# A GRU's first 20 steps take their input products on TensorE, and one prune moves from GpSimd to VectorE

## The chip, the cores and the metric

One core of one Trainium2 chip runs the whole program. The metric is device time of one execution in microseconds (us). The engines are named as in the profile: PE is TensorE (PEld its weight loads), DVE VectorE, ACT ScalarE, POOL GpSimd, SP SyncE; each runs its own queue of instructions in order and waits on semaphores that the others raise.

## The reference

Two blocks of attention and feed-forward; the change lies where the first block's feed-forward meets the GRU (a recurrent cell) of the second. `x` has 4 sequences (B) of 256 tokens (S) with 256 features (D).

```python
# first block's feed-forward, 2-of-4 sparse; I = 1024
h = silu(x @ w_gate) * (x @ w_up)
out = sparsify_2to4(h) @ w_down        # in each four, the two largest |h| stay
x = x + out
# GRU over the 256 tokens; state h: [4, 256]
gi = x_t @ W_ih + b_ih                 # depends on x alone: "input products"
gh = h @ W_hh + b_hh                   # depends on the step before
r = sigmoid(i_r + h_r); z = sigmoid(i_z + h_z); n = tanh(i_n + r * h_n)
h = (1 - z) * n + z * h                # 256 steps, one after the other
```

The attention and the routed feed-forward that follow are not touched.

## The kernel before

The feed-forward and the GRU run together. The tokens are cut into 8 tiles of 32 steps (each tile has 32 tokens of each of the 4 sequences). A tile goes through these stages, and each must be done before the GRU reaches the tile:

- `hidden_in(tile, n, up)`: gate (up = 0) or up product of half n (512 of the 1024 hidden features), two matmuls of 512 columns, into one of the PSUM banks a to d.
- `gate_sigmoid`, `gate_copy`, `up_copy` (ACT), then `multiplied` and `pruned`/`pruned_pool`: silu times up, then the 2-of-4 mask. In tile 0 DVE does it (`multiplied_at_once`, `pruned`). In tile 1 POOL multiplies both halves; DVE prunes the first half just before the GRU begins and POOL the second. In later tiles POOL does all of it.
- `by_hidden` (PE transposes), `by_hidden_out` (ACT copies them), `down` (PE, product with w_down), `grown` (DVE adds to xT, the tokens by feature).
- `rows_in` (PE): the tile's input products for r and z, by token; `rows_out` (DVE) adds the biases and writes them to SBUF; `spread`: 16 DMAs a tile move them into `g_row`, one row per step, in the layout that the steps want. SP issues 8 of tile 0's and ACT 8; of a later tile SP issues 12 and ACT 4. `cols_in` and `cols_out` do the same for n without DMAs.

Tile 0's stages, up to the landing of its 16 DMAs, stand in front of step 0. Those of the later tiles are fitted into the steps: after a step's three gates PE has one slot for an extra piece of work, and a step without such a piece has one `keep_warm` matmul there. DVE and ACT have such slots too. Which step has which piece is written out by the step's place u in its tile.

A step t, with what releases what:

- ACT has copied ("seeded", L1408) the input products of r and z and the bias of n into three banks. PE adds h @ W_hh (`gate`, L1324): for each of r, n, z 8 small matmuls (weights of 4 columns, 64 moving columns, four column groups side by side), 16 records in the profile, 48 a step.
- DVE transposes r (L1620), then n (L1624); ACT takes the sigmoid of r (L1448), then of z (`gate_z`, L1453), and then seeds r for the step after (`seed_r`). DVE: pre_n (L1629), transpose of z (L1631). ACT: tanh (L1457), then it seeds n and z (`seed_nz`), then its own extra piece. DVE: h (L1638), which releases PE's next step.

At a tile's first step `seed_r` waits until the tile's 16 DMAs have landed (g_g2).

## Time and profile before

| | us |
|---|---|
| median of 3 runs | 1009.99 (1008.89 to 1012.1) |
| profiled execution, its own time | 1006.44 |
| its span, first to last instruction | 1004.5 |
| PE busy | 798.6 (79%) |
| DVE busy | 609.5 (61%) |
| ACT busy | 477.3 (48%) |
| POOL busy | 414.2 (41%) |

The mean granted TensorE clock over the span is 0.962 of full speed. The busy shares are means over stages with different limits; in the GRU, which runs from 326.65 to about 815 us, no engine is full, and what counts is the loop from h to the next h. Times in the rows are us from the start of the span.

### The profile page before, as it was taken

Reading aid. Unit: us, or ns where it says so; the run is one execution under the profiler, and the core shown is the slowest. Engines: PE = TensorE matmul, PEld = TensorE weight load, DVE = VectorE, ACT = ScalarE, POOL = GpSimd, SP = SyncE. Lnnn points to the kernel's source line nnn. Section 1 sums busy time; section 2 is a strip of 40 time slices with the busy share of each in tenths; the row PEclk is TensorE's granted clock in tenths of the full one; section 3 lists DMA queues with packets and bytes.
Section 4 is the critical chain, followed back from the end, with each engine's and each line's share of the span. In section 5 each row is a group of like instructions: output and inputs, shape, how many; then the busy total and the mean of one; then the engine's idle time right before and its main releaser. Section 6 shows DMA issues by size and latency. Waiting matters only on the chain.

```text
span 1004.5 us, 39546 instructions
## 1 busy us (share of the span) xinstructions
PE 798.6 (79%) x16646; PEld 511.5 (51%) x16646; DVE 609.5 (61%) x2100; ACT 477.3 (48%) x1905; POOL 414.2 (41%) x493
## 2 busy tenths in 40 slices
PE   3789977868997886969779696886776678998876
PEld 3444544445654564645546464564544445566554
DVE  5655555786647676666767666676666643334347
ACT  2523433376642565656556565565544523344222
POOL 0385680374136394773928659095002002220000
PEclk9999999998999999999999999899989989999968
DMA  8100000400000000000000000000031000000001
GB/s 254 31 1 2 1 1 1 157 1 1 2 22 11 4 8 11 3 15 5 12 6 4 14 4 14 4 4 15 4 84 48 4 2 1 2 2 1 1 1 42
DMA packets 33343, 20.14 MB, mean 20 GB/s; under 512 B 23952, under 2 KB 30096, under 8 KB 33168
## 3 DMA queue, kind: packets, MB, share of 16 engines
q1 hardware_dynamic: 27984, 17.04, 6.1%
q8 instruction: 131, 2.15, 0.9%
q10 hardware_dynamic: 5184, 0.59, 0.4%
q14 instruction: 44, 0.36, 0.1%
HBM read 14.47 MB, written 1.05 MB: 15 GB/s over the span
## 4 chain that ended last, share of the span: by engine, by line
PE 52%; DVE 24%; ACT 8%; issue 6%; SPq 2%; DMA 2%; POOL 1%; ACTq 0%; DVEq 0%; POOLq 0%
PE banks L1324 15%; PE banks L1269 5%; DVE work L1624 4%; DVE h_ring L1638 3%; DVE gate_r L1620 3%; PE banks L1294 3%; ACT nzh L1457 3%; DVE pre_n L1629 3%; SPq L1249 2%; PE banks L410 2%; PE banks L1668 2%; PE banks L385 2%; PE banks L318 2%; PE banks L1750 2%; PE banks L1724 1%
## 5 line engine op out<-in xcount | busy, mean ns | idle before, releaser
L1324 PE MATMUL banks<-w_qkv,h_ring 128*4 128x64 f32 x12288 | 228.4, 224 | 111.9 <-DVE h_ring L1638 100.2
L1324 PEld LDWEIGHTS banks<-w_qkv,h_ring 128*4 128x4 f32 x12288 | 179.1, 89 | 214.9 <-DVE h_ring L1638 199.5
L1448 ACT ACTIVATE banks<-gate_r 128x8 f32<-128x8 f32 x256 | 46.2, 181 | 182.5 <-DVE gate_r L1620 181.7
L1620 DVE STREAM_TRANSPOSE gate_r<-banks 128x64 f32<-128x64 f32 x256 | 63.9, 250 | 80.2 <-PE banks L1324 76.3
L318 PE MATMUL banks<-zero 128*128 128x512 bf16 x285 | 97.8, 413 | 3.4 <-DVE work L2196 2.6
L1624 DVE STREAM_TRANSPOSE work<-banks 128x64 f32<-128x64 f32 x256 | 76.6, 299 | 2.7 <-PE banks L1324 2.5
L1638 DVE TENSOR_TENSOR_SCAN h_ring<-banks,nzh 128x24 f32<-128x24 f32 x256 | 52.9, 207 | 34.3 <-ACT nzh L1457 2.8
L1489 POOL TENSOR_TENSOR work<-work 128x512 f32<-128x512 f32 x14 | 17.8, 1270 | 122.8 <-ACT work L1385 122.8
L1629 DVE TENSOR_TENSOR_SCAN pre_n<-banks,work 128x16 f32<-128x16 f32 x256 | 48.7, 190 | 27.3 <-DVE work L1624 1.4
L1631 DVE STREAM_TRANSPOSE banks<-gate_z 128x64 f32<-128x64 f32 x256 | 60.4, 236 | 4.8 <-ACT gate_z L1453 3.7
L1457 ACT ACTIVATE nzh<-pre_n 128x8 f32<-128x8 f32 x256 | 54.5, 213 | 16.2 <-DVE pre_n L1629 1.4
L1453 ACT ACTIVATE gate_z<-banks 128x64 f32<-128x64 f32 x256 | 57.4, 224 | 9.3 <-PE banks L1324 9.3
L1565 POOL COPY probs_b<-h_ring 128x128 f32<-128x128 f32 x16 | 7.3, 486 | 125.5 <-DVE h_ring L1638 125.5
L1408 ACT COPY banks<-big 128x64 f32<-128x64 f32 x256 | 53.9, 211 | 9.8 <-DMA big<-big 9.8
L1408 ACT COPY banks<-grids 128x64 f32<-128x64 f32 x256 | 53.9, 211 | 0.8 <-DMA grids<-big 0.8
L1133 DVE TENSOR_REDUCE nraw<-banks 128x2 f32<-128x512 f32 x64 | 42.3, 686 | 19.3 <-PE banks L816 19.1
L1408 ACT COPY banks<-bhn 128x64 f32<-128x64 f32 x256 | 53.9, 211 | 0.0
L1588 DVE TENSOR_TENSOR nzh<-h_ring,banks 128x16 f32<-128x16 f32 x256 | 43.8, 171 | 11.0 <-ACTq L1444 1.8
L318 PEld LDWEIGHTS banks<-zero 128*128 128x128 bf16 x285 | 28.2, 102 | 38.3 <-issue 9.5
L1903 ACT ACTIVATE work<-banks 128x768 f32<-128x768 f32 x32 | 24.2, 808 | 38.0 <-PE banks L1750 38.0
L1294 PE MATMUL banks<-work,shared 128*128 128x128 f32 x256 | 36.4, 287 | 0.7 <-ACT work L1397 0.7
L645 POOL TENSOR_TENSOR rq<-nrm,half 128x64 f32<-128x64 f32 x3 | 31.7, 10577 | 12.0 <-DVE nrm L695 12.0
(436 smaller groups left out, 1654.1 us busy)
## 6 DMA issues: line engine op xcount, KB each, us to landing
big<-in_x SPq DMA_DIRECT2D x1, 1024.0 KB, 5.8
w_gate<-in_L_ffn_w_gate SPq DMA_DIRECT2D x1, 1024.0 KB, 5.0
shared<-in_L_ffn_w_down SPq DMA_DIRECT2D x1, 1024.0 KB, 7.5
w_gate<-in_L_ffn_W SPq DMA_DIRECT2D x1, 1024.0 KB, 7.4
shared<-in_L_ffn_W SPq DMA_DIRECT2D x1, 1024.0 KB, 11.3
out_x<-big SPq DMA_DIRECT2D x4, 256.0 KB, 2.4
w_qkv<-in_L_cond_W_qkv SPq DMA_DIRECT2D x1, 768.0 KB, 7.0
w_qkv<-in_L_attn_W_qkv SPq DMA_DIRECT2D x1, 768.0 KB, 8.7
```

What stands on the lines that cost most here:

```text
L318: nc.tensor.matmul(bank[:, :], zero16[:, 0:P], zero16[:, :], start=True, stop=True, skip_group_check=True)
L1269: mm = nc.tensor.matmul(bank[:, :], xg[:, tile, k, :], w_gate[:, k, n * 512:(n + 1) * 512] if not up else w_up[2 * k + n], start=(k == 0), ...
L1294: mm = nc.tensor.matmul(out[:, 0:P], w_down[:, c, m * P:(m + 1) * P], keptT[:, c, :], start=(c == 0), stop=(c == FC - 1), skip_group_check ...
L1324: mm = nc.tensor.matmul(bank[32 * j:32 * j + B, 0:64], h_col(t, c), w_hh[:, c, g, :].rearrange("p (m n) -> p m n", m=KC)[:, :, 32 * j:32 * ...
L1408: return nc.scalar.copy(bank[:, 0:64], rows).then_inc(done, 1)
L1453: nc.scalar.activation(gate_z[:, :], bank_z[:, 0:64], ACT.Sigmoid, scale=-1.0).then_inc(g_sz, 1)
L1457: nc.scalar.activation(every(nzh[:, :], 0, 3), every(pre_n[:, :], 1), ACT.Tanh, scale=-1.0).then_inc(g_th, 1)
L1620: nc.vector.transpose(gate_r[:, :], bank_r[:, 0:64]).then_inc(g_tr, 1)
L1624: nc.vector.transpose(blocks(npair[:, 16 * (t % RING):16 * (t % RING) + 128], 0), bank_n[:, 0:64].rearrange("p (m n) -> p m n", m=KC)).the ...
L1629: nc.vector.tensor_tensor_scan(pre_n[:, :], zr[:, :], npair[:, 16 * (t % RING):16 * (t % RING) + 16], 0.0, ALU.mult, ALU.add).then_inc(g_p ...
L1631: nc.vector.transpose(blocks(zz[:, :], 2, 3), gate_z[:, :].rearrange("p (m n) -> p m n", m=KC)).then_inc(g_tz, 1)
L1638: nc.vector.tensor_tensor_scan(h_ring[:, h_at(t + 1):h_at(t + 1) + 24], zz[:, 0:24], nzh[:, :], 0.0, ALU.mult, ALU.subtract).then_inc(g_h, 1)
```

## The change

Steps 0 to 19 (`DIRECT = 20`) no longer take their r and z input products from `g_row`. ACT seeds their banks with the bias alone (`bias_row`, four small DVE copies made once), and PE adds x_t @ W_ih with a new function, `inputs`: 8 matmuls of the same shape as a gate's, with token t's columns of xT as weights. For z they stand between gate n and gate z of the same step. For r they stand after gate z of the step before, ahead of the step's extra piece. So tile 0's `rows_in` move into the slots of steps 0 and 1, its `rows_out` to steps 3 to 6, and its 16 `spread` DMAs are all issued by SP; step 20 is the first that waits for them.

Tile 1's first half is now multiplied and compared on DVE before `grown`, counted after it, and its four last operations (`kept_of`) stand in steps 0 to 3. POOL multiplies and prunes only tile 1's second half, and not before h of step 0 is ready (g_h). The extra pieces of tile 0's steps are newly set: `by_hidden(1)` in steps 4 and 12, `hidden_in(2)` in 6 to 11, 13 and 14, and `down(1)`, `grown(1)`, `rows_in(1)`, `cols_in(1)`, `rows_out(1)` and tile 1's `spread` one step later than before (`late`). There are no keep_warm matmuls in steps 0 to 18 nor the 24 before step 0.

```diff
+            def inputs(t, bank, g, seed):
+                pe.wait_ge(seed, t + 1)
+                for c in range(KC):
+                    for j in range(4):
+                        nc.tensor.matmul(bank[32 * j:32 * j + B, 0:64], xT[:, c, t:t + (B - 1) * S + 1:S],
+                                         w_ih[:, c, g * D:(g + 1) * D].rearrange("p (m n) -> p m n", m=KC)[:, :, 32 * j:32 * j + 32],
+                                         start=False, stop=False, skip_group_check=True)
...
-            for k in range(KC):
-                rows_in(0, k)
-            cols_in(0)
+            pe.wait_ge(e_x2, 2)
             for bank in (bank_r, bank_n, bank_z):
                 mm = nc.tensor.matmul(bank[:, 0:64], zero16[:, 0:P], zero16[:, 0:64], start=True, stop=True, skip_group_check=True)
             mm.then_inc(g_open, 1)
-            keep_warm(24, bank_b)
+            cols_in(0)
+            inputs(0, bank_r, 0, g_sdr)
...
                 gate(t, bank_n, 2, g_sdn, g_nm)
+                if t < DIRECT:
+                    inputs(t, bank_z, 1, g_sdz)
                 gate(t, bank_z, 1, g_sdz, g_zm)
-                if u in (3, 4) and tile + 1 < TILES:
+                if t + 1 < DIRECT:
+                    inputs(t + 1, bank_r, 0, g_sdr)
+                if tile == 0 and u in (0, 1):
+                    rows_in(0, u)
+                elif tile == 0 and u in (4, 12):
+                    by_hidden(1, u // 12)
+                elif tile == 0 and u in (6, 7, 8, 9):
+                    hidden_in(2, 0, u // 8, [u % 2])
+                elif tile == 0 and u in (10, 11, 13, 14):
+                    hidden_in(2, 1, u < 12, [u - (10 if u < 12 else 13)])
...
-                else:
+                elif t + 1 >= DIRECT:
                     keep_warm(1, bank_b)
...
+            def row_of(t, g):
+                if t < DIRECT:
+                    return bias_row[:, 2 * g:2 * g + 2, :].rearrange("p m n -> p (m n)")
+                return g_row[t // TILE % 2][:, t % TILE, g, :]
...
             def seed_r(t):
-                if t % TILE == 0:
+                if t == DIRECT or t and t % TILE == 0:
                     act.wait_ge(g_g2, G2_DMAS * 16 * (t // TILE + 1))
...
-            for n in range(2):
-                multiplied(pool, nc.gpsimd, chain, 1, n)
+            pool.wait_ge(g_h, 1)
+            multiplied(pool, nc.gpsimd, chain, 1, 1)
             pruned_pool(pool, chain, 1, 1)
...
+            multiplied_at_once(v, chain, 1, 0)
+            compared(v, chain, 1, 0)
             for m in range(KC):
                 grown(0, m)
-            for n in range(4):
-                rows_out(0, n)
...
+            counted(chain, 0)
...
+                if tile == 0 and u < 4:
+                    kept_of(0, u)
+                if tile == 0 and u in (3, 4, 5, 6):
+                    rows_out(0, u - 3)
...
-                for j in range(2 if tile == 0 else 3):
+                for j in range(4 if tile == 0 else 3):
```

## Rows read from the trace of the kernel before

**Rows 1.** The page's costliest group: the gates (busy, mean ns of one | idle before).
```profile
L1324 PE MATMUL banks<-w_qkv,h_ring 128*4 128x64 f32 x12288 | 228.4, 224 | 111.9 <-DVE h_ring L1638 100.2
```

**Rows 2.** Timeline of PE ahead of step 0: start, length, what [idle <-releaser].
```profile
306.25 1.95 PE L1294 MATMUL banks<-work,shared 128*128 128x128 f32 x16
309.63 0.66 PE L1282 MATMUL banks<-cst,work 128*128 128x128 f32 x4 [1.43 <-DVE work L1512]
310.97 2.05 PE L1294 MATMUL banks<-work,shared 128*128 128x128 f32 x16 [0.68 <-ACT work L1397]
...
315.26 1.16 PE L1316 MATMUL banks<-xT,w_ih 128*128 128x128 f32 x8
...
326.65 1.46 PE L1324 MATMUL banks<-w_qkv,h_ring 128*4 128x64 f32 x48 [4.97 <-ACT banks L1408]
```

**Rows 3.** Timeline of DVE in the same stretch.
```profile
296.51 0.43 DVE L1501 TENSOR_SCALAR work<-work 128x512 int32<-128x512 int32 x1
...
297.45 0.42 DVE L1504 TENSOR_TENSOR c2p<-work 128x256 bf16<-128x256 f32 x1
...
298.20 0.49 DVE L1506 TENSOR_TENSOR win<-c1p 128x512 bf16<-128x512 bf16 x1
...
300.02 1.30 DVE L1512 SCALAR_TENSOR_TENSOR work<-win,work 128x128 f32<-128x128 bf16 x4
...
302.68 1.45 DVE L1501 TENSOR_SCALAR work<-work 128x512 int32<-128x512 int32 x1
...
304.64 1.49 DVE L1504 TENSOR_TENSOR c2p<-work 128x256 bf16<-128x256 f32 x1
...
313.06 0.29 DVE L1577 TENSOR_TENSOR xT<-banks,xT 128x128 f32<-128x128 f32 x1 [0.60 <-PE banks L1294]
```

**Rows 4.** Timeline of POOL: the first of tile 1's two multiplies.
```profile
302.57 1.27 POOL L1489 TENSOR_TENSOR work<-work 128x512 f32<-128x512 f32 x1 [9.52 <-ACT work L1385]
```

**Rows 5.** Timeline of ACT: the first seed.
```profile
326.30 0.22 ACT L1408 COPY banks<-big 128x64 f32<-128x64 f32 x1 [9.10 <-DMA big<-big]
```

**Rows 6.** Timeline, all engines: a step with keep_warm (step 5).
```profile
336.97 0.86 PE L1324 MATMUL banks<-w_qkv,h_ring 128*4 128x64 f32 x48 [0.40 <-DVE h_ring L1638]
...
337.76 0.39 PE L318 MATMUL banks<-zero 128*128 128x512 bf16 x1
337.89 0.22 ACT L1453 ACTIVATE gate_z<-banks 128x64 f32<-128x64 f32 x1
...
338.81 0.86 PE L1324 MATMUL banks<-w_qkv,h_ring 128*4 128x64 f32 x48 [0.66 <-DVE h_ring L1638]
```

**Rows 7.** Timeline, all engines: a step whose gate_z came late (step 70).
```profile
459.03 0.86 PE L1324 MATMUL banks<-w_qkv,h_ring 128*4 128x64 f32 x48 [0.65 <-DVE h_ring L1638]
...
460.14 0.22 ACT L1453 ACTIVATE gate_z<-banks 128x64 f32<-128x64 f32 x1 [0.17 <-PE banks L1324]
460.26 0.22 ACT L1408 COPY banks<-big 128x64 f32<-128x64 f32 x1
...
461.02 0.39 PE L1324 MATMUL banks<-w_qkv,h_ring 128*4 128x64 f32 x13
```

**Rows 8.** Timeline of PE: extra pieces down (step 14) and rows_in (step 19).
```profile
354.67 1.16 PE L1294 MATMUL banks<-work,shared 128*128 128x128 f32 x8
355.76 0.86 PE L1324 MATMUL banks<-w_qkv,h_ring 128*4 128x64 f32 x48
...
363.90 1.04 PE L1306 MATMUL banks<-w_ih,xT 128*32 128x512 f32 x8
```

**Rows 9.** Timelines of SP and ACT: tile 1's DMAs and the seed waiting for them.
```profile
372.83 10.44 SPq L1249 DMA_DIRECT2D grids<-big  x12
...
386.74 0.22 ACT L1408 COPY banks<-grids 128x64 f32<-128x64 f32 x1 [0.31 <-DMA grids<-big]
```

**Rows 10.** Windows (length, busy by engine, PEclk the granted clock): step 62, steps 0 to 19.
```profile
443.30:445.70 2.40, 2.00 (x49) 1.28 (x49) 1.36 (x7) 0.95 (x7) 2.32 (x4) 0.51 0.00 0
...
326.65:365.06 38.41, 34.34 (x1029) 22.16 (x1029) 25.58 (x123) 23.55 (x130) 21.73 (x28) 0.95 0.02 4
```

More of the change, by code:

```diff
@@ L1260, in hidden_in @@
                         pe.wait_ge(e_free, n + 1)
+                    elif tile == 2 and n == 0:
+                        pe.wait_ge(e_free, 3)
                     elif tile and up == 0:
@@ L1275, in by_hidden @@
                 pe.wait_ge(e_kept[n], tile + 1)
[L1276 removed]
+                if tile == 1 and n:
+                    pe.wait_ge(e_trc, 3)
+                elif tile and n == 0:
                     pe.wait_ge(g_nd, tile)
@@ L1354, in phase3_pe @@
                 tile, u = divmod(t, TILE)
+                late = 1 if tile == 0 else 0
                 pe.wait_ge(g_h, t + 1)
@@ L1444, in phase3_act @@
             act.sem_inc(g_act, 1)
+            for m in range(KC):
+                cols_out(0, m)
             for t in range(S):
                 tile, u = divmod(t, TILE)
+                late = 1 if tile == 0 else 0
                 act.wait_ge(g_tr, t + 1)
@@ L1491, in multiplied, with pruned, compared @@
             op.tensor_tensor(h, h, k, ALU.mult).then_inc(e_hid, 1)
-        def pruned(eng, chain, tile, n):
-            op = nc.vector
-            h, ab, k = (a[:, 512 * n:512 * (n + 1)] for a in (hid, sgm, kept))
-            one, two, three, w = (a[:, P * n:P * (n + 1), :] for a in (c1p, c2p, c3p, win))
-            if tile == 0:
-                eng.wait_ge(e_free, n + 1)
-            else:
-                eng.wait_ge(e_hid, 2 * tile + n - 1)
+        def pruned(v, chain, tile, n):
+            compared(v, chain, tile, n)
+            counted(chain, n)
+            for e in range(4):
+                kept_of(n, e)
+        def compared(v, chain, tile, n):
+            op = nc.vector
+            h, ab = (a[:, 512 * n:512 * (n + 1)] for a in (hid, sgm))
+            one, two, three = (a[:, P * n:P * (n + 1), :] for a in (c1p, c2p, c3p))
+            v.wait_ge(e_free, 2 * tile + n + 1)
             chain.done(op.tensor_scalar(ab.bitcast(I32), h.bitcast(I32), 0x7FFFFFFF, None, ALU.bitwise_and))
-            a4, h4 = quad(ab), quad(h)
+            a4 = quad(ab)
             op.tensor_tensor(one[:, :, 1:4], a4[:, :, 0:3], a4[:, :, 1:4], ALU.is_ge)
@@ L1505, in pruned, with counted @@
             chain.done(op.tensor_tensor(three, a4[:, :, 0:1], a4[:, :, 3:4], ALU.is_ge))
+        def counted(chain, n):
+            op = nc.vector
+            one, two, three, w = (a[:, P * n:P * (n + 1), :] for a in (c1p, c2p, c3p, win))
             chain.done(op.tensor_tensor(w, one[:, :, 1:5], one[:, :, 0:4], ALU.subtract))
```

105 lines of the change are left out of this document (56 added, 49 removed).

## The prediction

> **What bounds the kernel now.** I read the page first. Its costliest group is the GRU's gates: 228.4 us busy, and before them 111.9 us idle, 100.2 of it until h was ready [rows 1]. That is a sum over 256 steps, and the change lies in two places only: the run-up to step 0 and the GRU's first 32 steps. So I went on to the timelines of PE, DVE, POOL and ACT ahead of step 0 [rows 2 to 5]. What the reader is to see there: after tile 0's xT is complete (DVE, 313.06 + 0.29 = 313.35 [rows 3]) nothing is computed that step 0 waits for except the input products; then ACT waits 9.10 us for the DMAs that spread them, seeds at 326.30 [rows 5], and PE, idle for 4.97 us, begins step 0 at 326.65 [rows 2]. Then the steps: one with a late gate_z and one without, and those with an extra piece [rows 6 to 8]. In an ordinary step PE is not the bound, since its 48 records take 0.86 us [rows 6]; the loop h, r, n, pre_n, tanh, h is. But with `down` in the slot PE is: `down` starts at 354.67 and the next step's gates at 355.76, 1.09 later [rows 8]. The slot has no slack left there. Last, tile 1's DMAs and the seed that waits for them [rows 9], and the windows [rows 10].
>
> **The run-up.** Three things shorten it.
> (a) POOL no longer works beside DVE's second prune. The same DVE operations took 0.43 and 0.42 us alone (296.51, 297.45) and 1.45 and 1.49 (302.68, 304.64) while POOL multiplied [rows 3, 4]: 2.09 us. PE waited 1.43 us for that prune before `by_hidden` at 309.63; its preceding `down` half began at 306.25 and takes 1.95, of which the last 0.1 overlaps, so it can start at 308.1. I take 1.55 us; the other 0.5 is covered by PE.
> The Trainium skill ("GPSIMD Engine Reference", Key points) says that GpSimd's SBUF interfaces are shared with VectorE and collide with instructions in a 2-port mode or with two SBUF inputs. The two slow operations fit that; by this rule the rest of the prune loses nothing once POOL is silent, which is what the 2.09 assumes.
> (b) xT is complete at 313.35 - 1.55 = 311.8. Before that DVE fits `multiplied_at_once(1, 0)` (two operations, under 0.75 each) and `compared` (1.69, from 296.51 to 298.20 [rows 3]) in: 307.5 + 1.5 + 1.7 = 310.7, before `grown` can begin, so they cost nothing. If they were late, each us would come on top.
> (c) Behind xT DVE has only `counted`, 1.8 us (298.20 to 300.02 [rows 3]), and PE the opening matmuls, `cols_in` (1.16 [rows 2]) and `inputs` for r (below, 0.22), some 1.6 in all. DVE is the later one. With 0.1 for the semaphores step 0 starts at 311.8 + 1.8 + 0.1 = 313.7, against 326.65: **-12.95 us**. The DVE copies of `bias_row` go into a wait of DVE before its first multiply and are costed at nothing; without that cover they are under 1 us.
>
> **An `inputs` call.** There is none in this trace. Its matmuls have the gate's shape and count, so by the nearest row 16 records cost 16 x (0.86 - 0.22) / 47 = 0.22 us [rows 1, 6]. The token's four columns lie 256 elements apart instead of 6; that could make the weight load dearer. Bounds: nothing, and twice as much, 0.44. I take 0.22.
>
> **A step that has them.** Let s be the start of its gates. z is complete at s + 0.86 + 0.22 = 1.08, gate_z begins about 0.06 later (in step 5 it began at 0.92 [rows 6]): 1.14. A gate_z this late has an example: step 70 began at 459.03, gate_z at 460.14 (1.11), the seed of r at +0.12, and the next step at 461.02, 0.88 after gate_z [rows 7]. So a step without extra piece lasts 1.14 + 0.88 = 2.02 us.
> Now the queue. `inputs(t + 1)` for r is ahead of the extra piece on PE, and it waits for `seed_r(t + 1)`, which ACT does only behind gate_z: begun 1.14 + 0.12, 0.22 long, with a semaphore 1.52. Queued behind that wait is everything that PE has. PE is then busy with r's inputs (0.22), changes from column groups to the whole array, and starts the extra piece: records of a step last 0.64 to the last one's start, and the next kind starts at 337.76 - 336.97 = 0.79, so 0.15 for the change [rows 6]. Extra piece: 1.52 + 0.21 + 0.14 = s + 1.87, where it was s + 0.79. PE then decides the period:
> - `down` and `hidden_in` (of one length in this trace within 0.04): 1.87 + 1.09 [rows 8] = 2.96. Steps 6 to 11, 14 to 18: 11 x 2.96 = 32.56.
> - Step 13: `hidden_in(2, 1)` for bank c waits for `by_hidden_out(1, 1)`, which ACT does in the same step behind its seeds: about s + 1.8, 0.6 long. Starts 2.44, + 1.09 = 3.53.
> - `by_hidden`, 0.66 long [rows 2]: 1.87 + 0.66 = 2.53; steps 4, 12: 5.06.
> - `rows_in` keeps the column groups; 1.76 + 1.04, less 0.14 of overlap [rows 8] = 2.66; steps 0, 1: 5.32.
> - Steps 2, 3, 5, 19: 4 x 2.02 = 8.08.
> Sum 54.55, against 38.41 before [rows 10] (in which steps 0 and 1 ran at the half clock): **+16.1 us**. DVE's `kept_of` (about 0.33 each, a quarter of 1.30 [rows 3]) and `rows_out` stand in the slack before r's transpose or in PE-bound steps; without the cover 0.1 to 0.3 in step 3 alone. If `inputs` cost nothing the first 20 steps would still be 6 to 7 us longer than before, because the wait for the seed stays; at 0.44 it is 8 us worse than the sum.
> The Trainium skill ("TensorEngine Tiling (Array Packing)", Key Properties) has "Mode switching requires drain": the change of tiling drains the array. The 0.15 of rows 6 agrees. Without it the 11 steps would be about 0.15 shorter each, 1.6 us; this does not turn the sign.
>
> **Tile 1's DMAs.** SP's 12 issues take 10.44 us from 372.83, and ACT's seed for step 32 waits for them, 0.31, until 386.74 [rows 9]. `rows_out(1)` ends a step later, so SP starts a step later, and step 32 does not move with it: one ordinary step is added, which lasts 338.81 - 336.97 = 1.84 [rows 6]: **+1.84 us**. Bounds: SP's pace varies; 0.3 if the earlier arrival had slack of its own, 2.9 if it is slower. Tile 0's 16 DMAs, all on SP now at 0.87 each, start after `rows_out` in step 6 (about 330), are issued by 344 and landed by 348; step 20's seed comes at about 366. Nothing waits. The tile 1 prune on POOL, 21 operations of about 1.27 [rows 4] from 313.7, ends by about 340; `by_hidden(1, 1)` in step 12 wants it at about 346.
>
> **Sum.** -12.95 + 16.1 + 1.84 = +5.0 us. On the profiled execution that is 1006.44 + 5.0 = 1011.4, with a span of 1009.5; the median of the runs lies 3.55 above that execution, so 1009.99 + 5.0 = 1015.0. A measurement of this kernel tells apart about 0.3%, 3 us.
>
> **Rivals.**
> 1. *The seed wait is hidden* (the other side). If PE's slot were free enough that r's inputs and the extra pieces fit ahead of the next h, all 20 steps would last 2.02: 40.4, +2.0, total -12.95 + 2.0 + 1.84 = -9.1, 1000.9 us. For it: in a keep_warm step PE is idle for half of it. Against it: `down` already takes its slot to the end [rows 8]. It decides when the 16 steps with a piece lose under 0.5 us each instead of about 0.9. 15%.
> 2. *The DMAs do not come later for step 32*, and PE changes over faster: +5.0 - 1.6 - 1.5 = +1.9, 1011.9, within the 0.3%. 22%.
> 3. *The clock.* In step 62, clock 0.51, a step took 2.4 us instead of 1.84 [rows 10]. PE is idle nearly 3 us in the stretched step 31, and steps 2, 3, 5 lose their keep_warm. Four steps at the half clock more: +2.3, 1017.3. 15%. The other way, the two half-clock steps at the start are already counted as gone.
> 4. *The start does not move as far*, because `counted` or the copies on DVE come late: each us goes to the sum; +2, 1017. 8%.
> The forecast itself: 40%.
>
> **How the numbers follow.** Forecast, 3 and 4 are slower: 63%. Rival 2 is the same: 22%. Rival 1 is faster: 15%. The likeliest case alone has 1012.5 to 1017.5. The range is 1007.5 to 1019.0: from half-way to rival 1 (half of the seed wait hidden) to the clock and a dearer `inputs`; it leaves out rival 1 proper and the doubled price.
>
> **What the profile would show.** Step 0's gates at about 313.7 at full clock; DVE's operations of the second prune at 0.43 and 0.42; in steps 6 to 18 gates every 2.9 to 3.0 us, PE waiting for ACT's seed (L1408 group) behind gate z; gates of step 20 at about 368; ACT waiting some 2.1 us for DMAs in step 31; from step 32 on the same periods. The prediction is wrong if the steps with `hidden_in` last near 2.0 (the wait costs nothing), if `inputs` takes far from 0.22, or if step 0 starts after 316.

## The result and the profile after

The changed kernel took 1023.54 us, the median of 4 runs (1017.16 to 1027.07), beside 1009.44 (1006.13 to 1012.1) of the kernel before on the same chip: ratio 1.0129, 95% interval [1.008, 1.0179]. It is slower, as forecast, but by 14.1 us instead of 5.0, outside the range. Its profiled execution is 1023.6 with a span of 1021.8, so the two profiled spans differ by 17.3 us. Medians and ranges are of all executions; the ratios leave out those more than 1.5% above the fastest of their kernel. Divided at the gates of step 0, 20 and 32 and at the end of the GRU (a later start is +):

| stretch | before | after | difference | predicted |
|---|---|---|---|---|
| start of step 0 | 326.65 | 315.53 | -11.1 | -12.95 |
| steps 0 to 19 | 38.41 | 63.09 | +24.7 | +16.1 |
| steps 20 to 31 | 22.33 | 24.44 | +2.1 | +1.84 |
| steps 32 to 255 | 427.46 | 435.02 | +7.6 | 0 |
| behind the GRU | 189.65 | 183.72 | -5.9 | 0 |

The first `hidden_in` behind the attention began at 292.01 before and at 293.94 after, though PE's work ahead of it did not change; counted from there the start moved by 13.05. The -5.9 at the end is unchanged code too, with the granted clock at 0.92 before and 0.96 after. Both are differences between two executions, not the change.

**The run-up** came as worked out. PE, DVE and ACT, against [rows 2, 3, 5]:

```profile
309.97 0.60 PE L1287 MATMUL banks<-cst,work 128*128 128x128 f32 x4
...
314.85 0.41 PE L1329 MATMUL banks<-w_ih,xT 128*4 128x64 f32 x16
315.53 0.63 PE L1337 MATMUL banks<-w_qkv,h_ring 128*4 128x64 f32 x32 [0.27 <-issue]
```
```profile
304.62 0.43 DVE L1537 TENSOR_SCALAR work<-work 128x512 int32<-128x512 int32 x1
...
305.55 0.42 DVE L1540 TENSOR_TENSOR c2p<-work 128x256 bf16<-128x256 f32 x1
...
315.61 1.43 DVE L1555 SCALAR_TENSOR_TENSOR work<-win,work 128x128 f32<-128x128 bf16 x1
```

With POOL silent the two slow DVE operations are at 0.43 and 0.42, and PE no longer waits for them. Less the later start of 1.93, `by_hidden` is at 308.04 and step 0 at 313.60 (predicted 308.1 and 313.7). The last row is the new thing here: `kept_of`, which takes 0.33 a piece in a row of four when DVE is alone [rows 3], takes 1.43 beside POOL's first multiply (which now begins at 315.51), and r's transpose of step 0 is queued behind it.

**A step with inputs and `hidden_in`**, step 7, PE and ACT among all engines, against [rows 6]:

```profile
333.82 0.63 PE L1337 MATMUL banks<-w_qkv,h_ring 128*4 128x64 f32 x32
...
334.27 0.41 PE L1329 MATMUL banks<-w_ih,xT 128*4 128x64 f32 x16
...
334.50 0.41 PE L1337 MATMUL banks<-w_qkv,h_ring 128*4 128x64 f32 x16
...
334.97 0.22 ACT L1478 ACTIVATE gate_z<-banks 128x64 f32<-128x64 f32 x1 [0.20 <-PE banks L1337]
335.36 0.41 PE L1329 MATMUL banks<-w_ih,xT 128*4 128x64 f32 x16 [0.46 <-ACT banks L1433]
...
335.70 1.13 PE L1272 MATMUL banks<-w_gate,xnT 128*128 128x512 f32 x2
...
336.76 0.63 PE L1337 MATMUL banks<-w_qkv,h_ring 128*4 128x64 f32 x32
```

gate_z is at s + 1.15 (predicted 1.14), r's inputs at s + 1.54 (1.52), `hidden_in` at s + 1.88 (1.87), the next step at 2.94 (2.96). An `inputs` call of 16 records costs 334.50 - 334.27 = 0.23.

**What no row of before had led me to**: step 10 and those behind it. Timeline of PE:

```profile
343.09 0.63 PE L1337 MATMUL banks<-w_qkv,h_ring 128*4 128x64 f32 x30
346.25 0.22 PE L1337 MATMUL banks<-w_qkv,h_ring 128*4 128x64 f32 x1 [2.54 <-issue]
...
350.11 1.04 PE L1337 MATMUL banks<-w_qkv,h_ring 128*4 128x64 f32 x32
...
399.02 0.73 PE L1337 MATMUL banks<-w_qkv,h_ring 128*4 128x64 f32 x36 [0.65 <-DVE h_ring L1690]
401.38 0.60 PE L1337 MATMUL banks<-w_qkv,h_ring 128*4 128x64 f32 x12 [1.63 <-issue]
```

The gates r and n are 32 records together. Behind the 30th, in the middle of gate n, PE stands for 2.54 us, and the wait is put down to "issue", that is to nothing that the profile shows: the program has no semaphore between two matmuls of one gate. Step 31 has the same in the middle of gate z. The longest such wait of the GRU is in step 223, where SP loads weights for what follows:

```profile
776.63 1.45 PE L1337 MATMUL banks<-w_qkv,h_ring 128*4 128x64 f32 x43 [3.95 <-issue]
```

The windows of after (length, busy by engine, PEclk, DMA share, GB/s) are steps 0 to 19, the stretch behind the wait in step 10, steps 32 to 35, 32 to 255 and 64 to 255:

```profile
315.53:378.62 63.09, 48.72 (x1657) 32.26 (x1658) 31.52 (x131) 22.47 (x129) 44.79 (x49) 0.92 0.05 8
346.79:354.97 8.18, 7.29 (x110) 3.31 (x101) 2.29 (x11) 2.15 (x12) 6.10 (x5) 0.50 0.02 4
403.02:412.63 9.61, 7.48 (x198) 5.44 (x199) 5.49 (x24) 3.62 (x24) 0.91 (x2) 0.56 0.02 3
403.06:838.08 435.02, 309.56 (x11273) 218.53 (x11346) 289.18 (x1380) 241.89 (x1395) 194.40 (x229) 0.96 0.07 14
464.94:838.08 373.14, 261.15 (x9650) 185.23 (x9715) 247.32 (x1182) 206.29 (x1193) 156.81 (x185) 0.96 0.07 15
```

After both waits the granted clock is at its lower level, 1.2 GHz (0.50; 0.56 over steps 32 to 35, which end on the higher level): step 10 took 7.02, step 11 4.90, step 12 3.28, steps 32 to 35 2.38 to 2.41 instead of 1.84. And the gates' group shows the sum, the first row of after, the second of before (groups by line; the last part is what ended PE's idle time):

```profile
L1337 PE MATMUL banks<-w_qkv,h_ring 128*4 128x64 f32 x12288 | 236.1, 225 | 139.2 <-DVE h_ring L1690 122.1 <-issue 15.0
```
```profile
L1324 PE MATMUL banks<-w_qkv,h_ring 128*4 128x64 f32 x12288 | 228.4, 224 | 111.9 <-DVE h_ring L1638 100.2 <-ACT banks L1408 5.0 <-issue 4.9
```

4.9 us of "issue" stood in the trace of before. The page's group row shows only the first releaser, and I read that one.

**What the wait is.** The DMA view of steps 0 to 19, after and then before, has a queue of its own for instructions:

```profile
q1 hardware_dynamic: 2304, 0.26, 2.8%
q8 instruction: 13, 0.21, 1.7%
```
```profile
q8 instruction: 8, 0.13, 1.4%
```

The windows count 1657 matmuls and 1658 weight loads on PE in the first, 1029 and 1029 in the second [rows 10]: 3315/13 = 255 and 2058/8 = 257 instructions for each transfer, of 16384 bytes each. So PE's stream comes in blocks of 256. The Trainium skill ("Runtime: NRT & Kernel Launch", Instruction fetch mechanics) says the same of the blocks, 16 KiB of 256 instructions; it adds that crossing from one to the next is "mostly hidden", and here the traces disagree: 3.95 us of waiting for one in step 223, 14.8 us in nine waits in all.

### The profile page after: what moved, and what is told of

It is laid out like the page before. It is cut to its first block, busy times and chain, and to the rows that moved or that the text cites. A ratio compares the mean times of both kernels' runs of the same rounds, so it can differ in the third digit from the quotient of the medians.

```text
span 1021.8 us, 40683 instructions
## 1 busy us (share of the span) xinstructions
PE 778.4 (76%) x17169; PEld 517.4 (51%) x17257; DVE 610.6 (60%) x2106; ACT 475.1 (46%) x1903; POOL 410.2 (40%) x491
## 4 chain that ended last, share of the span: by engine, by line
PE 54%; DVE 22%; ACT 8%; issue 7%; SPq 2%; DMA 2%; POOL 1%; DVEq 0%; POOLq 0%; ACTq 0%
PE banks L1337 15%; PE banks L1272 6%; DVE work L1676 4%; PE banks L1299 3%; DVE h_ring L1690 3%; DVE gate_r L1672 3%; ACT nzh L1482 3%; DVE pre_n L1681 3%; SPq L1250 2%; PE banks L411 2%; PE banks L386 2%; PE banks L1720 2%; PE banks L1802 2%; PE banks L319 2%; PE banks L1776 1%
## 5 line engine op out<-in xcount | busy, mean ns | idle before, releaser
L1337 PE MATMUL banks<-w_qkv,h_ring 128*4 128x64 f32 x12288 | 236.1, 225 | 139.2 <-DVE h_ring L1690 122.1
L1337 PEld LDWEIGHTS banks<-w_qkv,h_ring 128*4 128x4 f32 x12288 | 182.8, 89 | 218.1 <-DVE h_ring L1690 188.3
L1482 ACT ACTIVATE nzh<-pre_n 128x8 f32<-128x8 f32 x256 | 54.5, 213 | 14.1 <-DVE pre_n L1681 0.6
L319 PE MATMUL banks<-zero 128*128 128x512 bf16 x168 | 54.9, 412 | 4.4 <-DVE work L2248 2.6
L1433 ACT COPY banks<-big 128x64 f32<-128x64 f32 x216 | 45.6, 211 | 0.2 <-DMA big<-big 0.2
L319 PEld LDWEIGHTS banks<-zero 128*128 128x128 bf16 x256 | 25.0, 101 | 34.3 <-issue 7.9
```

The source lines that it names most:

```text
L319: nc.tensor.matmul(bank[:, :], zero16[:, 0:P], zero16[:, :], start=True, stop=True, skip_group_check=True)
L1337: mm = nc.tensor.matmul(bank[32 * j:32 * j + B, 0:64], h_col(t, c), w_hh[:, c, g, :].rearrange("p (m n) -> p m n", m=KC)[:, :, 32 * j:32 * ...
L1433: return nc.scalar.copy(bank[:, 0:64], rows).then_inc(done, 1)
L1482: nc.scalar.activation(every(nzh[:, :], 0, 3), every(pre_n[:, :], 1), ACT.Tanh, scale=-1.0).then_inc(g_th, 1)
```

## The experiments

All ratios are to the kernel before, measured on the same chip beside the kernel. Its median there was 1007.20 us beside experiments 1 to 4, 1012.46 beside 5, 7 and the first kernel of 6, 1012.42 beside the second kernel of 6, 8 and 9, and 1013.33 beside 10; so compare experiments by their ratios (after: 1.0129), not by their times. A wait for instructions is one of over 0.3 us that is put down to "issue". The windows and rows are those of each kernel's profiled execution.

**1. The inputs behind the extra piece.** The wait for the seed is then covered by the piece.

```
@@ the PE queue, in each step t @@
-                if t + 1 < DIRECT:
-                    inputs(t + 1, bank_r, 0, g_sdr)
                 (keep_warm or the extra piece)
+                if t + 1 < DIRECT:
+                    inputs(t + 1, bank_r, 0, g_sdr)
```

> The changed kernel with the extra piece of a step ahead of the r inputs of the next step on PE, instead of behind them. Theory (wait for the seed ahead of the piece is what makes the steps long): the piece starts at s + 1.0 instead of s + 1.87, the period of steps 6 to 11 and 14 to 18 falls from 2.94 to 2.97 us to about 2.35, that of steps 0 and 1 to about 2.2: 11 x 0.6 + 0.8 = 7.4 us less, 1016 us. Rival (PE is simply given too much work in these steps, whatever its order): the period stays above 2.8 and the time within 2 us of the changed kernel's.

Measured: 1025.76 us (1020.06 to 1031.46, 4 runs), ratio 1.0192 [1.0124, 1.026]. A step with a piece and no wait for instructions lasts 2.29 to 2.37, which was expected. But the whole did not fall to 1016, because PE now lacks instructions in steps 2, 5, 8, 10, 13, 16, 19 and 21, and steps 0 to 19 last 60.10. The worst is in step 10, timeline of PE:

```profile
343.46 0.63 PE L1337 MATMUL banks<-w_qkv,h_ring 128*4 128x64 f32 x30
347.80 0.22 PE L1337 MATMUL banks<-w_qkv,h_ring 128*4 128x64 f32 x1 [3.70 <-issue]
```

So removing the seed wait alone buys nothing: a step of some 164 instructions in 2.32 us asks for a block every 3.6 us, and PE waits. In steps 2, 5, 13, 16 and 19 not one packet of another queue moved from the start of the block's transfer to the end of the wait: these waits, 0.42 to 0.95 us, need no DMAs beside them. In steps 8 and 10 tile 0's DMAs moved, and there they are 1.64 and 3.70.

**2. Fewer direct steps.**

```
-        RING, TILE, TILES, G2_DMAS, DIRECT = 64, 32, S // 32, 16, 20
+        RING, TILE, TILES, G2_DMAS, DIRECT = 64, 32, S // 32, 16, 14
```

> The changed kernel with DIRECT = 14 instead of 20, nothing else. In the changed kernel's trace the 16 DMAs of tile 0 are issued from 331.3 to 344.2, so step 14 can take its rows. Theory (PE's queue waits for ACT's seed ahead of the extra piece): steps 14 to 18 go from 2.94 and 2.97 us back to 1.84 and 1.88, step 19 from 2.02 to 1.84, 5.6 us less in all; so 1023.5 - 5.6 = 1018 us. Rival (the loss lies in what the change does to the later steps and in stalls of PE for instructions): the time stays within 2 us of the changed kernel's.

Measured: 1012.02 us (1009.42 to 1017.95, 10 runs), 1.0051 [1.0018, 1.0083]. Steps 14 to 18 are back at 1.84 to 1.88, steps 0 to 19 last 53.16. That is 9.9 us less than after, where five steps of 1.1 and step 19 by 0.2 would be 5.7. Step 10 took 5.57 instead of 7.02 (its wait 1.92 instead of 2.54), step 11 3.75 instead of 4.90 and step 12 2.46 instead of 3.28; step 5's wait is absent. The whole fell by more than the 5.6 us expected (by the ratios 7.9). Steps 32 to 255 took 429.37, 5.7 less than after, in code that is the same: another number of PE instructions stands ahead of it.

**3. Tile 0 without its spread DMAs.**

```
-                    act.wait_ge(g_g2, G2_DMAS * 16 * (t // TILE + 1))
+                    act.wait_ge(g_g2, G2_DMAS * 16 * (t // TILE))
...
-                for j in range(4 if tile == 0 else 3):
+                for j in range(0 if tile == 0 else 3):
```

> The changed kernel without tile 0's 16 DMAs (steps 20 to 31 then take whatever lies in g_row, so the values from step 20 on are not the reference's); all else the same. Theory A (PE was starved of instructions in step 10, 2.5 us, and ran at the half clock in steps 11 and 12, because instruction fetches and SP's DMAs share the 16 DMA engines): no gap in step 10, steps 10 to 12 at 2.9, 2.9, 2.5 us, some 7 us less, 1016 to 1017. Theory B (the 320 matmuls more are what starves PE, without any DMA): the gap comes again in the first 20 steps, the time stays within 2 us of 1023.5.

Measured: 1024.93 us (1017.13 to 1031.97, 4 runs), 1.0182 [1.0102, 1.0263]. No wait for instructions from step 0 to 30. Windows of steps 0 to 19 and 32 to 255:

```profile
317.68:372.93 55.25, 44.36 (x1657) 29.95 (x1658) 31.49 (x131) 22.48 (x129) 44.41 (x48) 1.00 0.02 4
396.79:834.62 437.83, 336.87 (x11346) 220.11 (x11346) 289.75 (x1380) 241.75 (x1395) 194.86 (x229) 0.95 0.07 14
```

Full clock and 55.25, where the prediction's sum was 54.55. As to the whole time the expectation missed: it did not fall by 7 us, in four executions. In the profiled one the 7.8 us gained in steps 0 to 19 were lost by a start of step 0 that is 2.2 later, 2.8 more in steps 32 to 255 and 4.6 more behind the GRU. And since step 10 can be without a wait with these DMAs in place (experiments 4 and 10), its absence here does not by itself show them as its cause.

**4. POOL starts four steps later**, so that `kept_of` of steps 0 to 3 has DVE for itself.

```
-            pool.wait_ge(g_h, 1)
+            pool.wait_ge(g_h, 5)
```

> The changed kernel with POOL beginning tile 1's second half after step 3 (g_h 5) instead of after h of step 0 (g_h 1). In the changed kernel's trace the DVE operation L1555 in step 0 took 1.43 us beside POOL's first multiply, against about 0.33 alone, and step 0 lasted 3.26 us. Theory: contention of the two engines; step 0 goes to about 2.65, some 0.6 to 0.8 us less in all, which is near what a measurement can tell: 1022.8. Rival (L1555 is long for another reason, the first step itself): it stays at 1.4.

Measured: 1020.49 us (1017.18 to 1025.01, 4 runs), 1.0143 [1.0092, 1.0194]. Timeline of DVE in step 0, and then the window of steps 0 to 19:

```profile
318.59 0.41 DVE L1555 SCALAR_TENSOR_TENSOR work<-win,work 128x128 f32<-128x128 bf16 x1
```
```profile
318.52:373.36 54.84, 44.73 (x1657) 30.13 (x1657) 29.61 (x131) 22.49 (x129) 42.69 (x47) 1.00 0.05 9
```

Step 0 is 2.62 instead of 3.26: 0.64 for the collision. By the ratios the whole is no faster than after. The rest of the gain, 7.6, is that step 10 has no wait this time, which I had not expected of this edit: the blocks and SP's DMAs (from 332.99 here, 331.32 in after) met otherwise.

**5. Half a block more, in the changed kernel and in the one before.** 64 matmuls on zeros in steps 23 to 30 (128 instructions with their weight loads) move every later cut of the stream by half a block. They were meant to add no wait, but they do: steps 20 to 31 took 27.03 us instead of 24.44 in after and 25.84 instead of 22.33 in before, with waits for instructions in steps 28 and 30.

```
+                    if tile == 0 and 23 <= u <= 30:
+                        for _ in range(8):
+                            nc.tensor.matmul(bank_b[:, 0:64], zero16[:, 0:P], zero16[:, 0:64], start=True, stop=True, skip_group_check=True)
```

> The changed kernel with 8 small matmuls (64 columns, zeros, into the keep_warm bank; 16 instructions) behind the keep_warm of each of steps 23 to 30, where PE is idle for over half a microsecond: 128 instructions more, none on the path. In the changed kernel and in the three variants of it with the same number of PE instructions the steps in which PE stood without an instruction from step 32 on are nearly the same ones (93, 123, 126, 155, 158, 190, 223). Theory (where the stream of PE's instructions is cut into 16 KB fetches decides which fetch meets SP's DMAs): with the stream shifted by half a fetch these steps change, and the sum of steps 32 to 255 moves by 3 us or more from the 435 us of the changed kernel. Rival (chance of the execution, or the steps themselves): the same steps are hit, and the sum stays within 2 us.

> The kernel before with the same 128 idle instructions in steps 23 to 30. Theory (cut of the stream): the stalled steps (157, 219, 225 before) change, and the time moves, most likely up by 2 to 6 us, with no work added to the path. Rival: nothing moves, within 2 us of the kernel before.

Measured: after with it 1018.06 (1016.12 to 1024.48, 4 runs), 1.0113 [1.0058, 1.0167]; before with it 1014.68 (1005.34 to 1026.76, 10 runs), 1.0023 [0.9981, 1.0066]. The waits moved in both: from step 32 on, in after from steps 93, 123, 158, 190, 220 and 223 to 62, 124, 157, 159, 221 and 224, in before from 60, 157, 219 and 225 to 62, 126, 156, 188, 191 and 226, besides the one in step 30. Steps 32 to 255 of after with it, and in before with it the longest wait, in step 30:

```profile
398.38:826.01 427.63, 305.16 (x11273) 215.10 (x11346) 288.48 (x1380) 242.14 (x1395) 194.79 (x229) 0.98 0.07 14
```
```profile
383.44 0.22 PE L1324 MATMUL banks<-w_qkv,h_ring 128*4 128x64 f32 x1 [0.42 <-DVE h_ring L1641]
385.92 1.46 PE L1324 MATMUL banks<-w_qkv,h_ring 128*4 128x64 f32 x47 [2.25 <-issue]
```

427.63 instead of 435.02 behind work that is added: where the cuts fall does matter in the later tiles of these executions. For the kernel before the same shift doubled the waits (10.2 us for 4.9), but steps 32 to 255 took 428.28 for 427.46, and its time changed by less than can be told. The expected 2 to 6 us did not come.

**6. Half of the inputs**, with the order of experiment 1 and with the order as it is. Only the first of the two halves of the sum over D is computed.

```
             def inputs(t, bank, g, seed):
                 pe.wait_ge(seed, t + 1)
-                for c in range(KC):
+                for c in range(1):
```

> The variant swap (extra piece ahead of the next step's r inputs) with each inputs call cut to its first half, 4 matmuls of 8; the second half of x's features is left out of the input products of steps 0 to 19, so the values are not the reference's. Theory (swap's steps were 2.3 us where PE had instructions, but PE stood 15 us without them, because 64 instructions more per step at that pace are more than the fetches bring): the stalls in steps 0 to 19 fall from about 12 us to under 4, the heavy steps last about 2.1 us, and the whole takes some 10 us less than swap, 1014. Rival (the stalls come with the order or the DMAs alone): they stay above 8 us and the time above 1020.

> The changed kernel in its own order with each inputs call cut to its first half, 4 matmuls of 8 (the second half of x's features is left out of the input products of steps 0 to 19, so the values are not the reference's). Without stalls the sum gives each step two times 0.11 us less: steps with hidden_in 2.72, with down 2.75, steps 0 to 19 about 50.5 us. Theory (the number of instructions starves PE): no gap in step 10, 50.5 to 51.5 us, the whole about 8 us under the changed kernel. Rival (the wait for the seed is the only loss, stalls are chance): a gap of 2 us or more comes again, 53 us or more.

Measured: swapped 1005.78 us (996.83 to 1015.5, 10 runs), 0.9943 [0.9902, 0.9984], steps 0 to 19 in 44.87, a step with a piece 2.07, as expected, and no wait for instructions over 0.3 us once step 0 has begun. The whole is 2.5% under experiment 1 by the ratios, where 10 us were expected. In the given order 1016.66 (1010.7 to 1025.62, 10 runs), 1.0074 [1.003, 1.0117]; its undisturbed heavy steps last 2.71 to 2.75, as expected, but steps 0 to 19 lasted 54.20 instead of the 50.5 to 51.5 expected: there is a wait for instructions of 1.14 in step 12, and the clock was at 0.50 from 332.06 to 335.47. So half of the inputs does not take all waits away. Swapped and halved, timeline of PE:

```profile
331.92 0.63 PE L1337 MATMUL banks<-w_qkv,h_ring 128*4 128x64 f32 x32
332.37 0.30 PE L1329 MATMUL banks<-w_ih,xT 128*4 128x64 f32 x8
...
332.82 1.13 PE L1272 MATMUL banks<-w_gate,xnT 128*128 128x512 f32 x2
333.87 0.30 PE L1329 MATMUL banks<-w_ih,xT 128*4 128x64 f32 x8
```

With fewer instructions the order is worth 54.20 - 44.87 = 9.3 us in these steps, and with all of them 3.0 (63.09 - 60.10). The order pays only where PE's instructions keep up. (The 54.20 holds the wait and the slow steps just named, so some 2 of the 9.3 are not the order's.)

**7. Ten direct steps only, and the rows prepared ahead of step 0**, so that tile 0's DMAs start in step 0 and no tile 1 arrival is late.

```
-        RING, TILE, TILES, G2_DMAS, DIRECT = 64, 32, S // 32, 16, 20
+        RING, TILE, TILES, G2_DMAS, DIRECT = 64, 32, S // 32, 16, 10
@@ PE, ahead of step 0 @@
+            for k in range(KC):
+                rows_in(0, k)
@@ DVE, ahead of step 0; each with its branch in the steps removed @@
+            for e in range(4):
+                kept_of(0, e)
+            for n in range(4):
+                rows_out(0, n)
@@ PE, ACT and DVE; the pieces of steps 4 to 16 a step earlier @@
-                late = 1 if tile == 0 else 0
+                late = 0
```

> Tile 0's rows_in and rows_out are put back ahead of step 0, kept_of too, so that its DMAs run in the first steps; only 10 steps take their input products directly (DIRECT = 10); tile 1's pieces stand where late = 0 has them (hidden_in in steps 5 to 10, 12, 13, by_hidden in 4 and 11). Theory, by the sums of the traces: step 0 starts 2.3 us later than in the changed kernel, 10.8 us earlier than before; steps 0 to 19 take 43.0 us against 38.4 before, +4.6; step 31 waits no longer than before. In all -6 us, 1001, if the stalls for instructions stay as before; each us of stalls more comes on top. Rival (the change's gain ahead of step 0 is always eaten by the inputs): not faster than 1007.

Measured: 1010.19 us (999.08 to 1015.66, 12 runs), 1.0019 [0.9982, 1.0057]. Steps 0 to 19 lasted 50.31, not the 43.0 expected. Timeline of PE, step 2:

```profile
323.37 0.40 PE L1329 MATMUL banks<-w_ih,xT 128*4 128x64 f32 x14
326.87 0.22 PE L1329 MATMUL banks<-w_ih,xT 128*4 128x64 f32 x1 [3.10 <-issue]
```

SP's DMAs ran from 319.39, and in this one trace the waits (3.10 in step 2, 1.59 in step 4) stand where they are. The expected 1001 was missed by 9 us.

**8. Tile 0's later pieces a step earlier.** The 20 direct steps stay.

```
@@ PE, ACT and DVE @@
-                late = 1 if tile == 0 else 0
+                late = 0
@@ PE; ACT's copies alike @@
-                elif tile == 0 and u in (4, 12):
-                    by_hidden(1, u // 12)
+                elif tile == 0 and u in (4, 11):
+                    by_hidden(1, u // 11)
```

> The changed kernel with tile 1's pieces one step earlier (late = 0; hidden_in in steps 5 to 10, 12, 13, by_hidden in 4 and 11), so that tile 1's DMAs are issued from step 24 as before. Theory of the third term: step 31 falls from 4.0 us to about 2.1, steps 20 to 31 from 24.4 to 22.5 us, steps 0 to 19 stay (apart from stalls), 1.9 us less, 1021.6. Rival (step 31 is long because PE lacks instructions, whatever the DMAs do): it stays above 3.

Measured: 1021.87 us (1015.33 to 1024.56, 4 runs), 1.0113 [1.0046, 1.018]. Timeline of PE, steps 31 and 32:

```profile
397.92 0.86 PE L1337 MATMUL banks<-w_qkv,h_ring 128*4 128x64 f32 x48 [0.98 <-DVE h_ring L1690]
...
400.13 0.86 PE L1337 MATMUL banks<-w_qkv,h_ring 128*4 128x64 f32 x48 [1.03 <-DVE h_ring L1690]
```

Step 31 lasts 2.21 (4.04 in after, 2.11 before) and step 32 runs at the full clock: the term of +1.84 is real and can be had back. In after PE's wait for instructions and the late DMAs fell together in step 31; experiment 2 has the DMAs alone, a step 31 of 4.56 us without a wait for instructions. ACT's seed in it:

```profile
393.23 0.22 ACT L1433 COPY banks<-grids 128x64 f32<-128x64 f32 x1 [2.76 <-DMA grids<-big]
```

The whole moved by less than can be told; steps 0 to 19 lasted 61.93, with 0.71 and 3.63 us of waits.

**9. The kernel before with POOL's multiply behind DVE's prune**, and then also with the row of keep_warm matmuls long enough to reach step 0.

```
@@ POOL, ahead of its first multiply @@
+            pool.wait_ge(e_kept1, 1)
@@ PE, the second kernel only @@
-            keep_warm(24, bank_b)
+            keep_warm(44, bank_b)
```

> The kernel before with one edit: POOL begins tile 1's two multiplies only when DVE has pruned tile 0's second half (it waits for e_kept1). Term (a) of the sum alone: the two slow DVE operations fall from 1.45 and 1.49 us to 0.43 and 0.42, by_hidden starts 1.55 us earlier, step 0 too, 1.5 us less in all (0.15%, less than the timing can tell, so the trace has to show it). Rival (another engine or a DMA held them up): they stay at 1.4.

> quiet with 44 instead of 24 keep_warm matmuls ahead of step 0, so that PE is busy through the whole wait for tile 0's DMAs. Theory: the clock stays full, steps 0 and 1 last 1.84 us instead of 2.4, another 1.1 us less than quiet, 2.6 less than before (0.26%). Rival: the clock falls all the same, or the matmuls reach beyond the landing of the DMAs and step 0 starts later.

Measured: 1007.87 (998.17 to 1013.26, 12 runs), 0.9965 [0.9926, 1.0004], and 1007.25 (1001.4 to 1013.13, 12 runs), 0.997 [0.9938, 1.0003]. Timeline of DVE in the first; windows of steps 0 to 19 in the first and in the second:

```profile
303.81 0.43 DVE L1501 TENSOR_SCALAR work<-work 128x512 int32<-128x512 int32 x1
...
304.75 0.42 DVE L1504 TENSOR_TENSOR c2p<-work 128x256 bf16<-128x256 f32 x1
```
```profile
326.26:364.68 38.42, 32.74 (x1026) 22.17 (x1030) 25.59 (x123) 23.56 (x130) 21.89 (x28) 0.95 0.02 4
```
```profile
327.62:364.86 37.24, 31.51 (x1026) 21.13 (x1030) 25.31 (x123) 23.68 (x130) 21.58 (x28) 1.00 0.02 4
```

From the first `hidden_in` to step 0 it took 33.12 us instead of 34.64 in the first: -1.52, where the prediction took 1.55. The longer row has the clock at 1.00 in step 0 (-1.17 us) and ends 0.36 too late for it. Either is the best kernel here that computes everything, by 0.3%, and neither can be told from the kernel before.

**10. SP's DMAs of tiles 2 to 7 taken away**, in both kernels.

```
-                    act.wait_ge(g_g2, G2_DMAS * 16 * (t // TILE + 1))
+                    act.wait_ge(g_g2, 16 * (16 * min(t // TILE + 1, 2) + 4 * max(t // TILE - 1, 0)))
...
-                for j in range(4 if tile == 0 else 3):
+                for j in range((4, 3, 0, 0, 0, 0, 0, 0)[tile]):
```

> This is the changed kernel in which SyncE no longer spreads the gates of tiles 2 to 7 (72 of its 100 DMAs; ScalarE's own 4 in each tile stay, and so do all DMAs of tiles 0 and 1). It leaves out that part of the computation: the steps from 64 on read old gates. Nothing changes on TensorE. Theory A (a block of TensorE's instructions comes late when its transfer meets the packets of SyncE's spread DMAs): the steps of tiles 0 and 1 stall as in the changed kernel (step 10, step 31), but from step 64 to 255 nearly all of the waits for instructions go; steps 32 to 255 last 421 to 425 us instead of 435.0, the whole is 8 to 13 us faster than the changed kernel, ratio to the kernel before about 1.000 to 1.005. Theory B (the instruction stream stalls where it is cut, whatever the DMAs do): the stalls in steps 93, 123, 158, 190, 220 stay, steps 32 to 255 last 433 to 437 us, and the ratio stays at 1.01 to 1.018.

> This is the kernel before with the same edit (SyncE spreads only tiles 0 and 1; the steps from 64 on read old gates). Its waits for instructions in the profile were steps 60 to 62, 157, 219 and 225, 4.9 us with slow steps after each. Theory A (transfers of instructions are held up by the spread DMAs): from step 64 on they go, steps 32 to 255 last 421 to 425 us instead of 427.5, and the whole is 2 to 6 us faster, ratio 0.994 to 0.998; and the difference between the two kernels of this pair is about that of the first 32 steps alone, 12 to 17 us. Theory B: steps 32 to 255 stay at 427 to 429 us, ratio 0.999 to 1.002.

Measured: 1006.08 us (998.96 to 1012.32, 8 runs), 0.9924 [0.9886, 0.9963], and 998.77 (997.59 to 1002.07, 4 runs), 0.9868 [0.9812, 0.9924]. Windows of the changed kernel with the edit, steps 0 to 19 and 64 to 255, and then of the kernel before with it, steps 64 to 255:

```profile
315.61:370.85 55.24, 44.30 (x1657) 30.01 (x1658) 31.36 (x131) 22.73 (x129) 44.53 (x48) 1.00 0.05 9
456.00:814.72 358.72, 274.51 (x9715) 180.11 (x9715) 245.72 (x1183) 208.17 (x1194) 156.84 (x185) 1.00 0.05 13
```
```profile
453.90:813.59 359.69, 276.85 (x9715) 181.42 (x9715) 245.87 (x1183) 207.94 (x1194) 156.87 (x185) 0.99 0.05 13
```

From step 64 on the changed kernel has one wait left (1.65 us, at 746) and the other two (1.79 and 0.38, at 742 and 750), all where SP loads weights: from 742 to 750 its queue alone takes 93.2% of the DMA engines. Steps 32 to 255 last 419.86 and 419.08 (421 to 425 were expected), and steps 64 to 255 358.72 and 359.69; with the DMAs it was 373.14 and 366.81 (448.04 to 814.85): the edit is worth 14.4 us there in the changed kernel and 7.1 in the one before, and with it the two kernels are alike within 1 us. Not all of this is the spread DMAs. SP loads weights behind them, in after from 766.27 on, and with the edit from 739.00, so the edit moves that too. Up to step 218 there are spread DMAs alone; windows of steps 64 to 218, after and then with the edit:

```profile
464.94:762.65 297.71, 220.46 (x7856) 154.97 (x7904) 200.91 (x961) 171.17 (x974) 151.31 (x178) 0.97 0.04 8
456.00:743.93 287.93, 229.42 (x7902) 150.77 (x7902) 199.46 (x962) 172.71 (x975) 151.34 (x178) 1.00 0.04 9
```

That is 9.8 of the 14.4 us (and 293.38 - 286.97 = 6.4 of the 7.1). The other 4.6 lie in steps 219 to 255, where after has the longest wait, 3.95 us, while SP's queue takes 95.2% of the DMA engines (768 to 777): the next block's transfer began 12.6 us after the one before it. So of the 7.6 us of steps 32 to 255, 4.3 came where the blocks meet the spread DMAs, 2.0 from step 219 on, and 1.2 in steps 32 to 63, of which steps 32 to 35 are at the lower clock.

Three parts of the expectation failed. Steps 0 to 19 of the changed kernel took 55.24 with no wait in step 10, though up to step 63 every engine's work is that of after, DMAs included. So the wait in step 10 can stay away with nothing changed ahead of it: it is one way in which an execution can go. And the pair differs by 1006.08 - 998.77 = 7.3 us, not 12 to 17: that is nearly the prediction's +5.0. Third, by the ratios both kernels fell by more than was expected: the changed one by 2.0%, some 20 us (8 to 13 were expected), the one before by 1.3%, some 13 us (2 to 6). The traces of steps 64 to 255 show 14.4 and 7.1 us; what made up the rest is open.

**How late a block comes.** For each wait of over 0.3 us put down to "issue" in the GRU I took, in all sixteen traces, the time from the landing of the last instruction transfer to PE's next matmul. In the 27 cases in which at most 20 packets of the other queues moved in between it has a median of 1.4 us (1.2 to 2.2); in the 92 others of 3.0, and up to 5.4. In step 10 of after the transfer took from 340.60 to 342.50, and PE went on at 346.25, 3.75 later. The DMA view of that stretch, 340.2 to 346.3:

```profile
q1 hardware_dynamic: 864, 0.10, 10.8%
q8 instruction: 1, 0.02, 1.9%
```

864 packets of six spread DMAs and one of instructions. Two transfers of instructions never began closer than 3.25 us in the GRU of any trace. A step with inputs and no piece (160 instructions in 2.02 us) wants one every 3.2 us, the swapped order every 3.6, a step with `hidden_in` every 4.6, an ordinary step of before (98 in 1.84) every 4.8. The first would need blocks closer together than any two transfers came. The swapped order has its waits of 0.42 to 0.95 us, and step 5 of after its 0.65, without a packet of another queue; the long wait in step 10 of after, and three of the four waits of before, stand beside spread packets, the fourth (step 225, 1.81 us) beside SP's weight loads. No run shows what the fastest supply is.

## Why the prediction was wrong in its size

- **(a), the prune**: right, with POOL's rows as the cause (experiment 9: -1.52, predicted -1.55).
- **(b), (c), the start**: right within 0.1 us, counted from the same point. The copies of `bias_row` cost nothing.
- **An `inputs` call**: 0.22 to 0.23, predicted 0.22; the stride of 256 elements costs nothing that shows. One side sum beside it does not add up: without the cost of `inputs` the 20 steps come to 54.55 - 7.9 = 46.6, some 8 us over before, not 6 to 7; no term rests on it.
- **A step that has them**: right to 0.06 in each kind: 2.02, 2.94 to 2.97, 3.49, 2.47 to 2.52, 2.62. The queued wait for the seed is the mechanism. The Trainium skill ("TensorE: Matmul & The Clock Gate", Part 3, "What overlaps and what doesn't") has matmuls start and end in program order; step 7 agrees: `hidden_in`, ready long before, starts at 335.70 behind the inputs that waited until 335.36. At a finer scale it does not hold everywhere: behind the wait in step 10 three records of inputs start from 346.26 on, ahead of a record of gate n at 346.31 that stands before them in the program. Swapping the two takes the wait out (experiments 1 and 6).
- **`kept_of` and `rows_out` at 0.1 to 0.3 us, in step 3**: the cover was named, but not POOL. `kept_of` beside POOL's multiply costs 0.64 in step 0. In (a) I had the same collision by number and did not apply it where the change starts POOL's work anew.
- **Tile 1's DMAs**: the mechanism was right, and given back by experiment 8. The size, +1.84 forecast and 1.93 measured, is in part luck: in experiments 2 and 6 (swapped) step 31 took 4.56 and 4.91, 2.4 and 2.8 over before. PE lacked instructions in step 31 at the same time, and the half clock of steps 32 to 35 behind it is 2.3 us.
- **The step that failed** is that of the sum of steps 0 to 19, with its sentence "Nothing waits" on tile 0's DMAs, and the "from step 32 on the same periods". PE's supply of instructions stood at nothing in both, without a reason. The runs show in its place waits for late blocks and the lower clock behind them: the change uses 1.6 times as many blocks in steps 0 to 19 (13 for 8), puts tile 0's DMAs among them, and moves every later cut of the stream. The missing term was 8.5 us in steps 0 to 19 (63.09 - 54.55) and 7.6 in steps 32 to 255 in the profiled execution. With SP's later DMAs away in both kernels (10) their medians differ by 7.3 us instead of 14.1.
- **Rival 3**, the clock, came true where it looked, in steps 32 to 35 at 2.3 us, behind PE's idle time in step 31. In experiment 2 the same happens with no wait for instructions: PE idles 3.38 us in step 31, and steps 33 and 34 take 2.41. What it did not name is the lower clock behind waits for instructions, in steps 10 to 12 and later; behind the short one in step 5 the clock stayed full.
- **Rivals 2 and 4** are refuted: tile 1's DMAs come later, the extra piece starts at s + 1.88 (1.87), and step 0 is where it was forecast.
- **Rival 1** is refuted as the change is (the seed wait is not hidden), and comes near only if the inputs stand behind the piece and are half as many: 0.9943.

Shown is: the lack of instructions in the later tiles all but goes when SP's DMAs of these tiles go (10), and it moves with the cut (5). Not shown is that tile 0's moved DMAs made the wait in step 10: it stands beside them in after, but taking them away did not make the whole faster (3: 1.0182). Open is how often an execution of after has that wait. Five traces have its 20 direct steps, its order of inputs and piece, and tile 0's DMAs (after, experiments 4, 5, 8 and 10); a wait of over 1 us is in two of them (63.09 and 61.93 us for steps 0 to 19) and not in three (54.84, 56.62, 55.24). The 14.1 us between the medians are then 5.0 predicted and some 9 of this kind. Experiment 10 puts about 7 of the 9 (14.1 - 7.3) to the later tiles, with an uncertainty of several us, since its two ranges (998.96 to 1012.32 and 997.59 to 1002.07) overlap; more can't be read from one trace for each kernel. What happens between the landing of a block and PE's next matmul, in 1.4 or in 3 us, no row shows.

## What to carry to other kernels

Count the instructions that PE needs per microsecond, and ask what else the DMA engines do in that stretch; where a wait stands between two matmuls of one accumulation with "issue" as releaser, read it before anything else, in the groups by line and not only on the page. A piece of work that is moved for the sake of its dependencies also moves what it collides with: here 16 small-packet DMAs onto the steps with the densest instruction stream (what they cost there stayed open), and POOL's first multiply onto DVE's new work in step 0. And put an operand wait behind work that is ready, not ahead of it, but check that the instructions keep up, or the slot that it frees is lost again.

## What the runs showed of the hardware

- PE's instructions come by DMA, 256 in a transfer of 16384 bytes, and two transfers in the GRU began no closer than 3.25 us in sixteen traces. Spread DMAs with 144 packets each, under 512 bytes, move beside them: with no other queue's packets about, the waits in the swapped order were up to 0.95 us, with them up to 3.70; beside SP's weight loads, at 95.2% of the DMA engines, 3.95.
- Behind such a wait the granted clock often fell to 0.50: from 346.68 to 356.92 in after, behind 2.54 us of standing; but only from 350.12 to 353.53 in experiment 8, behind 3.63, and not at all behind the 0.65 us in step 5 of after. Steps 10 to 12 of after lost 6.75 us in all against their sizes of 2.96, 2.96 and 2.53, so 4.2 came behind the wait.
- Steps 0 to 19 of the same work took 63.09 in one kernel's execution and 55.24 in another's, and behind 128 added instructions that do nothing a stretch of 224 unchanged steps took 427.63 us instead of 435.02.
- DVE's operation on 128x128 elements that takes 0.41 by itself (experiment 4) takes 1.43 beside POOL's 128x512 f32 multiply.
